# The order of the steps of TensorE, VectorE, ScalarE and GpSimd, laid out anew, in a two-layer graph attention kernel

## The reference: what is computed

```python
def layer0(x, adj):                      # 6 heads of 64
    q, k, v = heads(x @ Wq + bq), heads(x @ Wk + bk), heads(x @ Wv + bv)
    probs = softmax(q @ k.T / sqrt(64) + where(adj, 0, -9e15))
    return merge(probs @ v) @ Wf + bf

def layer1(x, adj):                      # 12 heads of 32
    h = einsum('bnd,ade->bane', x, W)
    th = tanh(h)
    attn = (th @ w_src) + swap(th @ w_dst)          # one number a node and head, each
    attn = where(attn >= 0, attn, 0.2 * attn)
    attn = softmax(where(adj, attn, -999.0))
    f = elu(attn @ h + b)
    gate = sigmoid(x @ H_w.T + H_b)
    return gate * f + (1 - gate) * x

x = layernorm(x + layer0(x, adj))
x = layernorm(x + layer1(x, adj))
```

## Time and profile before

| | |
|---|---|
| median of 3 runs | 1223.84 us (1223.67 to 1231.86) |
| profiled execution | 1226.67 us, its span 1224.7 us |
| mean granted TensorE clock | 0.951 |
| busy share of TensorE, VectorE, GpSimd, ScalarE | 92%, 72%, 56%, 51% |
| DMA | 30.94 MB, mean 25 GB/s |

### The profile page before, as it was taken

The page is one execution under the profiler, slowest core; times in us unless marked ns, Lnnn a source line. Parts: engine busy times, 40 slices in busy tenths (PEclk is TensorE's granted clock), DMA queues, the critical chain, the costliest instruction groups (busy, mean ns, idle before and its releaser), DMA issues.

```text
span 1224.7 us, 24638 instructions
## 1 busy us (share of the span) xinstructions
PE 1129.6 (92%) x7407; PEld 1001.1 (82%) x7407; DVE 885.6 (72%) x2288; ACT 621.9 (51%) x1996; POOL 688.7 (56%) x605
## 2 busy tenths in 40 slices
...
DMA packets 34718, 30.94 MB, mean 25 GB/s; under 512 B 15872, under 2 KB 34688, under 8 KB 34688
## 3 DMA queue, kind: packets, MB, share of 16 engines
...
...
## 4 chain that ended last, share of the span: by engine, by line
PE 62%; DVE 16%; issue 12%; ACT 7%; POOL 2%; SPq 1%; DMA 0%; DVEq 0%; ACTq 0%; POOLq 0%
PE p_bank L472 41%; PE context L620 7%; ACT probs L689 5%; DVE weights L907 5%; PE scores L533 4%; PE t_bank L609 3%; PE context L554 2%; PE t_bank L580 2%; PE t_bank L542 2%; DVE neg_max L825 1%; DVE cT L785 1%; PE t_bank L600 1%; DVE x L855 1%; DVE stats L844 1%; DVE sum L936 1%
## 5 line engine op out<-in xcount | busy, mean ns | idle before, releaser
L1010 POOL TENSOR_TENSOR w_rows<-qwT,own_head 96x1536 fp32r<-96x1536 f32 x64 | 176.1, 2751 | 187.0 <-ACT qwT L750 187.0
L907 DVE SCALAR_TENSOR_TENSOR weights<-t_bank,pqw,clip 128x128 f32<-128x128 f32 x768 | 215.0, 344 | 38.0 <-PE t_bank L609 35.6
L620 PEld LDWEIGHTS context<-h,weights 128*128 128x128 f32 x1536 | 204.4, 203 | 6.4 <-DVE weights L907 1.5
L620 PE MATMUL context<-h,weights 128*128 128x33 f32 x1536 | 199.6, 279 | 0.8 <-DVE weights L907 0.8
L689 ACT ACTIVATE probs<-masked,neg_max 128x128 f32<-128x128 f32 x384 | 148.7, 390 | 34.5 <-DVE neg_max L825 34.5
L1003 POOL TENSOR_TENSOR prod<-th,w_sd 128x768 f32<-128x768 f32 x64 | 117.0, 1828 | 86.7 <-ACT th L717 86.7
L991 POOL TENSOR_TENSOR probs<-probs,rden 128x768 f32<-128x768 f32 x64 | 98.3, 1537 | 100.1 <-DVE rden L830 100.1
L472 PE MATMUL p_bank<-w_f,cT 128*128 128x384 f32 x576 | 120.5, 354 | 13.7 <-DVE cT L785 13.7
L878 DVE TENSOR_REDUCE sd<-prod 128x24 f32<-128x768 f32 x64 | 60.6, 947 | 92.0 <-POOL prod L1003 92.0
L472 PE MATMUL p_bank<-w_g,x1T 128*128 128x384 f32 x576 | 123.6, 362 | 0.0
L472 PE MATMUL p_bank<-w_h,x1T 128*128 128x384 f32 x576 | 120.4, 355 | 2.6 <-DVE x1T L785 2.6
...
## 6 DMA issues: line engine op xcount, KB each, us to landing
...
```

The source lines that it names most:

```text
L620: last = te.matmul(context1[:, n * (HD1 + 1):(n + 1) * (HD1 + 1)], weights[:, n, :], h[:, g % 2, n, :], start=True, stop=True)
L907: last = dve.scalar_tensor_tensor(out=weights[:, n, :], in0=src[:, i * P:(i + 1) * P], scalar=pqw[:, g % 2, 0, n:n + 1], in1=clip[:, g, :] ...
L1010: pool.tensor_tensor(w_rows[0:QW_ROWS, k % 2], over_heads(qwT[:, k % 2, 1, :].bitcast(F32), H1), per_head(own_head[:], P), ALU.mult).then_ ...
```

## The change

The twelve tables of steps (four engines in the stages first, loop and last) are written anew. Nothing else changes: the same steps, the same instructions, semaphores, tiles and sizes, and the same list for SyncE. The banks of single steps change, as they follow from the order. Of the diff, one table:

```diff
 PE_LOOP = [
-    ("v", 0), ("x1T", 0), ("qk", 0), ("qk", 1), ("x1T", 1), ("h", 0), ("gate", 0), ("qk", 2), ("qk", 3), ("qwT", 0),
...
+    ("x1T", 0), ("qk", 0), ("v", 0), ("qk", 1), ("x1T", 1), ("h", 0), ("gate", 0), ("qk", 2), ("qk", 3), ("qwT", 0),
...
 ]
```

More of the change, by code:

```diff
@@ L27 @@
 PE_LOOP = [
[8 rows of a table removed]
[8 rows of a table added]
 ]
 ACT_LOOP = [
[L38 to L42, removed]
@@ L43 @@
-    ("pTo", 5), ("gatet", 2), ("chi", 1), ("exp", 3), ("elu", 2), ("chi", 2), ("vout", 3), ("pTo", 6), ("xhi", 0),
-    ("pTo", 7), ("xhi", 1), ("elu", 3), ("chi", 3), ("gatet", 3), ("xhi", 2), ("xhi", 3),
+    ("x1hi", 0), ("qkout", 0), ("vout", 0), ("qkout", 1), ("hout", 0), ("masks", 0), ("x1hi", 1), ("pqw", 0),
+    ("gatet", 0), ("qwhi", 0), ("qkout", 2), ("qwTo", 0), ("qkout", 3), ("hout", 1), ("qkout", 4), ("pqw", 1),
+    ("qwhi", 1), ("qkout", 5), ("qwTo", 1), ("x1hi", 2), ("gatet", 1), ("exp", 0), ("hout", 2), ("exp", 1),
@@ L45 @@
+    ("x1hi", 3), ("elu", 0), ("pTo", 0), ("vout", 1), ("pqw", 2), ("qwhi", 2), ("pTo", 1), ("hout", 3), ("qwTo", 2),
+    ("pTo", 2), ("chi", 0), ("exp", 2), ("pTo", 3), ("vout", 2), ("elu", 1), ("pqw", 3), ("gatet", 2), ("qwhi", 3),
+    ("chi", 1), ("qwTo", 3), ("vout", 3), ("exp", 3), ("pTo", 4), ("pTo", 5), ("chi", 2), ("xhi", 0), ("elu", 2),
+    ("pTo", 6), ("pTo", 7), ("xhi", 1), ("chi", 3), ("xhi", 2), ("elu", 3), ("xhi", 3), ("gatet", 3),
 ]
 DVE_LOOP = [
-    ("x1lo", 0), ("gsum", 0), ("sd", 0), ("sda", 0), ("wlog", 0), ("qwlo", 0), ("x1lo", 1), ("sd", 1), ("e", 0),
@@ L48 @@
[L48 to L57, removed]
@@ L58 @@
-    ("stats0", 3), ("sum1", 3), ("mv0", 3), ("out", 2), ("stats1", 3), ("mv1", 3), ("x1", 2), ("clip", 1), ("x1", 3),
+    ("x1lo", 0), ("gsum", 0), ("sd", 0), ("sda", 0), ("x1lo", 1), ("wlog", 0), ("qwlo", 0), ("e", 0), ("sd", 1),
+    ("sda", 1), ("wlog", 1), ("qwlo", 1), ("gsum", 1), ("x1lo", 2), ("mask", 0), ("max", 0), ("e", 1), ("e", 2),
+    ("mask", 1), ("e", 3), ("rden0", 0), ("max", 1), ("rden1", 0), ("f_raw", 0), ("e", 4), ("sd", 2), ("rden0", 1),
+    ("sda", 2), ("gsum", 2), ("x1lo", 3), ("mask", 2), ("e", 5), ("wlog", 2), ("mixa", 0), ("mixb", 0), ("qwlo", 2),
@@ L59 @@
+    ("sum1", 0), ("stats1", 0), ("rden1", 1), ("max", 2), ("f_raw", 1), ("sd", 3), ("clo", 0), ("mask", 3),
+    ("sda", 3), ("rden0", 2), ("max", 3), ("e", 6), ("wlog", 3), ("e", 7), ("qwlo", 3), ("mixa", 1), ("mixb", 1),
[4 rows of a table added]
+    ("out", 1), ("mv1", 2), ("gsum", 3), ("x1", 1), ("xlo", 3), ("clip", 0), ("sum0", 3), ("mixa", 3), ("stats0", 3),
+    ("mv0", 3), ("mixb", 3), ("sum1", 3), ("stats1", 3), ("x1", 2), ("mv1", 3), ("out", 2), ("x1", 3), ("clip", 1),
     ("out", 3),
@@ L61 @@
 POOL_LOOP = [
[L62 to L65, removed]
+    ("prod", 0), ("rows", 0), ("prod", 1), ("rows", 1), ("x_res", 0), ("prod", 2), ("norm", 0), ("fb", 0),
```

49 lines of the change are left out of this document (24 added, 25 removed), and 38 rows, old and new, of tables (DVE_FIRST, DVE_LOOP, PE_FIRST, PE_LAST).

## The result

The changed kernel takes 1132.95 us (median of 4 runs, 1132.33 to 1133.29), the kernel before 1223.81 us beside it (4 runs, 1223.67 to 1231.86). The measured ratio is 0.9236, 95% interval 0.9207 to 0.9264 (the quotient of the two medians, 0.9258, lies inside it): 7.6% faster, where 5.5% was forecast. The profiled execution took 1132.33 us, its span 1130.3 us, its mean clock 0.981 instead of 0.951: 94.3 us less than the profiled one of before.

What follows compares the result with a forecast made beforehand. TensorE, busy 92%, was taken to set the pace, with waits and clock falls on top. From 1226.7 us: 37.5 turns, 13 clock, 5 first stage, 12 last stage gave 1159.2, less 2.8 for the median: 1156 us, range 1132 to 1192.

Steps and rivals of the forecast that it cites:

- A turn at full clock: Loop turn of four graphs: 70.40 us falls by 2.5 to 67.9, in 15 turns 37.5 us, bounds 0 to 60.
- all five waits: TensorE's waits in a turn, qwT 2, wb 6, pT 3, wb 7 and f 3: 4.0 us of loss go.
- the seam: Between two turns: TensorE's x1T 0 waits for VectorE's clip 0, 0.8 us a turn, bounds 0.3 and 3.0.
- I take two thirds as gone, 13 us: Stretches at clock 0.50 cost 19 us in 15 turns; 13 us of it go, bounds 0 and 19.
- three pv1 with nothing larger between: TensorE's loop order: 3.5 us of three pv1 and three wb precede a clock fall; s 1 and two wb divide them.
- The first stage: TensorE waits some 6 us there, longest 1.5 for clip 0; w_h's later conversion saves 5 us, bounds 0 and 7.
- The last stage: 78.1 us with TensorE waiting for rows, e and qwlo; the new lists save 12 us, bounds 0 and 20.
- Moved waits: Rival: GpSimd's holds on VectorE move waits instead of removing them; 2 us a turn, 1186 us, range 1172 to 1205; chance 0.20.
- both tosses: VectorE against GpSimd: sda 2 with norm 1, sum1 1 with rows 3; the walk has VectorE starting first in both.
- The ring at the seam: Rival: VectorE's late tail delays TensorE, which delays the next turn; 1231 us at 5 us a turn; slower, chance 0.04.
- The clock rival that gained: Rival: clock never falls in the loop, last stage gets more upper level, about 1140 us; better than forecast, 1125 to 1140: 0.10.
- the hold of qwlo and sda: VectorE steps reading two SBUF tiles held until GpSimd's instruction ends: 1.29 and 1.12 us, to become 0.18.

Runs made afterwards that it cites:

- split_pv1: The kernel before with s 1 moved from behind wb 4 to between pv1 0 and pv1 1 in TensorE's loop table: 1239.41 us, ratio 1.0108.
- loop_new: The kernel before with the four tables of the loop changed alone, first and last stage as before: 1149.17 us, ratio 0.9351.
- first_new: The kernel before with the four tables of the first stage changed alone: 1219.27 us, one run.
- qwhi_early: The kernel before with ScalarE's qwhi 2 moved from behind hout 3 to directly behind pqw 2 in the loop: 1213.78 us, ratio 0.9844.
- pv0_late: The changed kernel with TensorE's pv1 0 moved behind s 1, directly ahead of pv1 1, in the loop: 1152.63 us, ratio 0.939.
- qwhi_back: The changed kernel with ScalarE's qwhi 2 put behind hout 3 again in the loop: 1155.47 us, ratio 0.9423.
- cover_s1: The changed kernel with pv1 0 directly ahead of pv1 1 and s 1 ahead of wb 1 in TensorE's loop table: 1152.37 us, ratio 0.9392.

## Why the prediction was right in direction and too small

**A turn at full clock: the term was mis-sized, 2.5 us where 3.5 were measured.** What was to go went, all five waits (4.0 us; 70.40 less the 66.33 of TensorE's work is 4.1). What was to come, 0.15 for h 1, 0.3 for the second pT, 0.8 for the seam and 0.25 for restarts, 1.5 us together, came as 0.6 us, all of it at the seam; the walk had put waits where there were none. 15 turns of about 1.0 us each are some 15 of the 26.9 us by which the profiled sum (1159.2 against 1132.33) missed.

**The clock: the step that failed was "I take two thirds as gone, 13 us".** It took one row as the pattern of all falls, and put what they cost at the loop's 1.27 us in each of the 15 turns, 19 us, which was also its upper bound. All went, and they had cost more: 16.5 us in the 13 turns, and as an estimate 2.9 in the second stage (one fall of 6.8 us, at the loop's 73.3 - 70.4) and 4.5 in the drain (one of 10.2 us, at split_pv1's 75.8 - 71.33). That is 24 us, 11 more than forecast. The cause stated, three pv1 with nothing larger between, was half of it: split_pv1 removed those falls and left the others. There is a second place, at the waits, which the prediction mentioned in half a sentence. The new order has no fall at either.

The Trainium skill, "TensorE: Matmul & The Clock Gate", section "HAM oscillation — how this bites in real kernels", was weighed as the rule that no order of this loop touches the clock. The runs decide against that use of it: tables alone (loop_new) kept the clock at 1.00 through all turns. For the falls behind waits its direction, pauses of TensorE, fits the row of 2.19 us in 3.50; for those behind the pv1 it does not, with 3.50 of 3.50.

**The first stage** gave 8.1 us where 5 were forecast, 6.0 of them by its own tables (first_new), a fall of the clock that is gone among them, and 1.6 only because x1T 0 now stands ahead of v 0; the term had neither. **The last stage** gave 9.6 where 12 were: the waits for rows and e shrank from 4.9 and 3.7 to 1.2 and 1.1 us, as said, but that for qwlo did not shrink, 4.2 in place of 3.5 (2.8 of it for qwT 3), and that for clip went from 3.3 to 4.4, most likely since clip 1 is now the second to last step of VectorE's tail. The clock there is 0.68, not 0.61. The median lies 0.6 us above the profiled run, not 2.8 below; with 26.2 for the turns, +3.1 and -2.4 for the ends, and 3.4 less for this, the miss is the 23 us between 1156 and 1133.

**The rivals.** Moved waits: both tosses fell as walked, sum1 1 (510.07 in the trace) just ahead of rows 3 (510.59). A hold did move, to wlog 3, but VectorE idles 0.2 us at 513.98 behind it, so it stays off the path. The ring at the seam didn't close in the loop: clip 1 is in time there. The clock rival that gained, "never falls in the loop", given with about 1140, is what happened.

**What was read rightly:** the hold of qwlo and sda and its release (1.29 and 1.12 us to 0.17 and 0.18), 1.25 us a turn from ScalarE's qwhi 2 moved alone (qwhi_early), the floor of 66.4 us, VectorE at 76%, x_res at no cost.

**What stays open.** How the moment at which a turn comes and the steps in it together bring the clock down (7 of 15 turns in pv0_late, 3 of 15 in qwhi_back), and why fewer falls come as longer ones (split_pv1), no run here settles; nor whether moving s 1 alone ends the falls (cover_s1 has another turn length), nor whether s 1 and pv1 together are enough without any wait, as pv0_late had one of 0.66 us 2 us ahead of them. How much of the new order's steady clock is due to the divided pv1 and how much to the waits that are gone isn't separated either. What put clip 1 late in the last stage was read from the new trace and not tried.
